# A fused Mamba, mixture-of-experts and attention kernel: the first scan's first B rows from TensorE, tables loaded ahead, filler products, orders set anew

## What is computed

```
x = x + mamba(layernorm(x))     # per sequence, a scan over 256 positions
x = x + moe(layernorm(x))       # router, top 2 of 8 experts
x = x + gated_attention(layernorm(x))
x = x + moe(layernorm(x))       # the same weights again
```

```
xn = x * rsqrt(mean(x * x) + 1e-6) * norm_scale
hidden, gate = split(xn @ in_w + in_b)
h = silu(causal_conv4(hidden) + conv_b)
ts, B, C = split(h @ xproj_w)              # 64, 16 and 16 columns
delta = softplus(ts @ dt_w + dt_b)
state_n[t] = exp(A_n * delta[t]) * state_n[t-1] + delta[t] * h[t] * B_n[t]
y[t] = sum_n C_n[t] * state_n[t] + D * h[t]
out = (y * silu(gate)) @ out_w + out_b
```

## Time and profile before

| | |
|---|---|
| median of 3 runs | 618.04 us (617.25 to 619.10) |
| the profiled execution | 618.93 us |
| its span in the trace | 617.1 us |
| TensorE granted clock, mean of the span | 0.986 |
| busy: TensorE, DVE, ScalarE, GpSimd | 595.6, 496.4, 396.9, 384.1 us |

### The profile page before, as it was taken

One profiled execution on the slowest core, in us unless ns is written; L12 is line 12 of the kernel. 1 busy time (PEld: TensorE's weight loads), 2 busy tenths in 40 slices (PEclk: granted clock), 3 DMA queues, 4 the chain that ended last, 5 costly groups with the idle time before them and its releaser, 6 DMA issues.

```text
span 617.1 us, 13011 instructions
## 1 busy us (share of the span) xinstructions
PE 595.6 (97%) x4502; PEld 550.9 (89%) x4502; DVE 496.4 (80%) x1077; ACT 396.9 (64%) x849; POOL 384.1 (62%) x360
## 2 busy tenths in 40 slices
PE   7779999799999999999999999999999999999997
PEld 6534886599999999999999999899999999999997
DVE  5796799788999899987999889898989895455444
ACT  5987777377677766867587767686676633616240
POOL 1494574579686997699678977697768773001000
PEclk9779999999999999999999999999999999999999
DMA  8763213101212204120404021210422000000000
GB/s 281 269 156 136 82 71 139 68 14 72 74 78 90 70 4 150 50 110 3 150 2 141 21 86 66 90 72 4 148 66 95 1 14 11 13 1 14 1 22 10
DMA packets 18466, 45.43 MB, mean 74 GB/s; under 512 B 2847, under 2 KB 13664, under 8 KB 14178
## 3 DMA queue, kind: packets, MB, share of 16 engines
q1 hardware_dynamic: 18402, 44.61, 21.0%
HBM read 40.15 MB, written 1.31 MB: 67 GB/s over the span
## 4 chain that ended last, share of the span: by engine, by line
PE 87%; POOL 3%; ACT 3%; issue 3%; DVE 2%; DMA 0%; SPq 0%; DVEq 0%; ACTq 0%; POOLq 0%
PE ps L1265 25%; PE ps L1069 14%; PE ps L1070 13%; PE ps L1071 13%; PE ps L1204 5%; PE ps L1314 2%; PE ps L1118 2%; POOL st L511 1%; POOL yacc L524 1%; PE ps L1084 1%; PE ps L1139 1%; PE ps L1064 1%; PE ps L1233 1%; PE ps L1326 1%; PE ps L1161 1%
## 5 line engine op out<-in xcount | busy, mean ns | idle before, releaser
L511 POOL TENSOR_TENSOR st<-st,rows_ring 128x512 f32<-128x512 f32 x128 | 164.0, 1285 | 85.6 <-DVE st L949 85.5
L1265 PE MATMUL ps<-down,inner_ring 128*128 128x128 f32 (+1 forms) x1408 | 171.5, 275 | 0.0
L1265 PEld LDWEIGHTS ps<-down,inner_ring 128*128 128x128 f32 (+1 forms) x1408 | 165.6, 191 | 2.6 <-issue 1.7
L750 ACT ACTIVATE sg<-ps 128x512 f32<-128x512 f32 x176 | 104.6, 596 | 82.5 <-PE ps L1071 72.5
L949 DVE TENSOR_TENSOR_SCAN st<-dA,ps 128x512 f32<-128x512 f32 x128 | 154.9, 1212 | 2.3 <-PE ps L1204 1.2
L1018 DVE TENSOR_TENSOR inner_ring<-sg,ps 128x512 f32<-128x512 f32 x176 | 119.1, 678 | 43.3 <-PE ps L1071 23.4
L524 POOL TENSOR_TENSOR yacc<-yacc,st 128x512 f32<-128x512 f32 x96 | 124.8, 1300 | 4.2
L698 ACT ACTIVATE dA<-delta,A 128x255 f32<-128x255 f32 x256 | 104.7, 495 | 0.2
L1069 PE MATMUL ps<-xhi,up_hi 128*128 128x256 f32 x352 | 103.9, 295 | 0.1
L1071 PE MATMUL ps<-xhi,up_lo 128*128 128x256 f32 x352 | 99.8, 283 | 0.0
L1070 PE MATMUL ps<-xlo,up_hi 128*128 128x256 f32 x352 | 99.7, 283 | 0.0
(11 more groups left out here) (150 smaller groups left out, 864.3 us busy)
## 6 DMA issues: line engine op xcount, KB each, us to landing
rows_ring<-bc SPq DMA_DIRECT2D x31, 1024.0 KB, 5.3
moved_rows<-inner_ring SPq DMA_DIRECT2D x96, 32.0 KB, 1.9
inner_ring<-gate_w SPq DMA_DIRECT2D x1, 1408.0 KB, 7.3
inner_ring<-up_w SPq DMA_DIRECT2D x1, 1408.0 KB, 10.0
down<-down_w SPq DMA_DIRECT2D x2, 512.0 KB, 10.4
out<-X SPq DMA_DIRECT2D x8, 128.0 KB, 1.9
rows_ring<-bc SPq DMA_DIRECT2D x1, 768.0 KB, 5.6
X<-x SPq DMA_DIRECT2D x1, 768.0 KB, 9.8
```

The source lines that it names most:

```text
L511: nc.gpsimd.tensor_tensor(st[:, i % NST], st[:, i % NST], row, ALU.mult).then_inc(s["m_p"], 1)
L750: nc.scalar.activation(sg[:, k % 2], two(bank_of(q, 2 * j)), ACT.Silu).then_inc(s["f_sg"], 1)
L1265: ins = nc.tensor.matmul(bank_of(q, 2 * NP + e)[:, c * H:(c + 1) * H], act_in, down[0:rows, e, n, :], start=n == 0, stop=n == NB - 1)
```

## The change

It changes five things in the code and all constants of the plan.

1. **B rows.** A new TensorE step `b_pe` takes, for states 0 and 1, the state's B column of `xproj_w` broadcast over 128 columns as the weights and h as the data, so the B row comes out on all 128 partitions in `rot[0]`. `dbx` of these two states copies it to SBUF (`b0`) first and no longer waits for the DMA; `mulC` of them waits for it, and the first sum waits until `rot[0]` is copied.
2. **Tables.** Two ScalarE steps, `t_soft` and `t_exp`, that only load a table.
3. **Fillers.** More in `m_turn` and `m_xp`, new ones before `m_dt` 0, `m_turn` 1, `m_ph` 1, `m_cv` 1 and before the sums 1 to 8 of sequence 0.
4. **Weight halves.** The second half of the weights' columns, which the first pairs use, is split first, and the first products wait for that half alone.
5. **Orders.** New constants, so new orders on every engine.

The code (the constants' tables but `TAPS` and `WARM` are left out; the orders that they give follow):

```diff
+NB0 = 2
+UP_PART = (3, 2, 0, 1)
...
-TAPS = {"split_in": 50.762, "lo_in": 60.743, "split_rows": 162.496, "lo_rows": 164.634, "h_table": 69.291}
-WARM = {"m_turn": 8, "m_ph": 2, "m_xp": 3, "sum": 2, "out": 6}
+TAPS = {"split_in": 37.063, "lo_in": 58.879, "split_rows": 161.491, "lo_rows": 172.175, "h_table": 65.824, "b_pe":
+        83.888, "t_soft": 75.704, "t_exp": 79.139}
+WARM = {"m_turn": 11, "m_ph": 2, "m_cv": 0, "m_xp": 5, "m_dt": 3, "turn1": 4, "ph1": 7, "cv1": 8, "early": 3, "sum":
+        2, "out": 6}
...
         delta = sb("delta", [P, 2, IT, T])
+        b0 = sb("b0", [P, NB0, T])
         rows_ring = sb("rows_ring", [P, NCH * CH * 2 * T])
...
                     pool.wait_ge(s["w_uh"], k // 2 + 1)
-                    cols = slice(k * HALF // 2, (k + 1) * HALF // 2)
+                    cols = slice(UP_PART[k] * HALF // 2, (UP_PART[k] + 1) * HALF // 2)
                     nc.gpsimd.tensor_tensor(up_lo[:, cols], up_raw[:, cols], up_hi[:, cols].bitcast(F32),
...
                 pool.wait_ge(s["m_scan"], i + 1)
+                if u == 0 and n < NB0:
+                    pool.wait_ge(s["d_r0" if n else "d_rf"], 16)
                 row = rowsbc[:, (i // CH) % NCH, n % CH, 1:2, :].broadcast_to([P, IT, T])
...
                     act.wait_ge(s["d_gate"], 16)
-                    half = slice(k * HALF, (k + 1) * HALF)
+                    half = slice((1 - k) * HALF, (2 - k) * HALF)
                     nc.scalar.copy(gate_hi[:, half], gate_raw[:, half]).then_inc(s["w_gh"], 1)
...
                     act.wait_ge(s["d_up"], 16)
-                    half = slice(k * HALF, (k + 1) * HALF)
+                    half = slice((1 - k) * HALF, (2 - k) * HALF)
                     nc.scalar.copy(up_hi[:, half], up_raw[:, half]).then_inc(s["w_uh"], 1)
...
                     dve.wait_ge(s["w_gh"], k + 1)
-                    half = slice(k * HALF, (k + 1) * HALF)
+                    half = slice((1 - k) * HALF, (2 - k) * HALF)
                     nc.vector.tensor_tensor(gate_lo[:, half], gate_raw[:, half], gate_hi[:, half].bitcast(F32),
...
                 dve.wait_ge(s["m_dx"], u + 1)
-                if i == 0:
-                    dve.wait_ge(s["d_rf"], 16)
+                if i < NB0:
+                    dve.wait_ge(s["m_b0"], i + 1)
                 else:
...
                 row = rowsbc[:, g % NCH, n % CH, 0:1, :].broadcast_to([P, IT, T])
+                if i < NB0:
+                    nc.vector.tensor_copy(b0[:, n], two(rot[0])[:, n]).then_inc(s["m_bc"], 1)
+                    dve.wait_ge(s["m_bc"], n + 1)
+                    row = b0[:, n:n + 1, :].broadcast_to([P, IT, T])
                 nc.vector.tensor_tensor(states_in(u, n), dxps, row, ALU.mult).then_inc(s["m_dbx"], 1)
...
                     dve.wait_ge(s["f_dn"], NE * (q - 1) + last_reader(j) + 1)
+                elif j >= RP + 2:
+                    dve.wait_ge(s["w_ul"], 4)
                 nc.vector.tensor_tensor(inner[:, j], sg[:, k % 2], two(bank_of(q, 2 * j + 1)), ALU.mult).then_inc(s["f_in"], 1)
...
+            summed = []
+
+            def fill(count):
+
+                if not summed:
+                    free("chain")
+                    warm(chainps, count)
+                elif summed[-1] < NS - 1:
+                    add_zeros(rot[0], count)
+
             def m_turn(u):
...
                     warm(chainps, WARM["m_turn"])
+                elif u == 1:
+                    fill(WARM["turn1"])
                 free(bank_name(u))
...
                     warm(chainps, WARM["m_ph"])
+                elif u == 1:
+                    fill(WARM["ph1"])
                 free(bank_name(u))
...
                     return
+                fill(WARM["cv1" if u else "m_cv"])
                 pe.wait_ge(s[f"w_diag{0 if u else 1}"], 1)
...
+            def b_rows(_):
+
+                pe.wait_ge(s["d_xpw"], 16)
+                pe.wait_ge(s["m_h"], 1)
+                for n in range(NB0):
+                    for it in range(IT):
+                        col = xpw[:, it, 96 + 2 * n:97 + 2 * n].broadcast_to([P, P])
+                        ins = nc.tensor.matmul(two(rot[0])[:, n], col, h[:, it], start=it == 0, stop=it == IT - 1)
+                    ins.then_inc(s["m_b0"], 1)
+
             def m_dt(u):
                 if u == 0:
+                    fill(WARM["m_dt"])
                     pe.wait_ge(s["d_dtw"], 16)
...
                     pe.wait_ge(s["m_y0"], u + 1)
+                    if u == 0:
+                        pe.wait_ge(s["m_bc"], NB0)
                     nc.tensor.matmul(two(rot[0]), ident[:], yacc[:, u % 2], start=True, stop=False)
+                summed.append(n + u * NS)
                 if n > NS // 2:
                     add_zeros(rot[0], WARM["sum"])
+                elif n and u == 0:
+                    add_zeros(rot[0], WARM["early"])
                 pe.wait_ge(s["m_p"], i + 1)
...
                     pe.wait_ge(s["m_scan"], NS)
-                    pe.wait_ge(s["w_gl"], 2)
+                    pe.wait_ge(s["w_gl"], 1)
                 elif q == 0 and 2 * j < NR0:
...
                     pe.wait_ge(sem, value)
+                if q == 0 and j == RP:
+                    pe.wait_ge(s["w_gl"], 2)
                 if j:
...
                 if q == 0 and j == 0:
-                    pe.wait_ge(s["w_ul"], 4)
+                    pe.wait_ge(s["w_ul"], 2)
                     pe.wait_ge(s["m_delta"], 2)
...
                     pe.wait_ge(sem, value)
+                if q == 0 and RP <= j < RP + 3:
+                    pe.wait_ge(s["w_ul"], 3 if j == RP else 4)
                 products(bank_of(q, 2 * j + 1), (up_hi, up_lo), q, j).then_inc(s["f_U"], 1)
```

94 lines of the change are left out of this document (47 added, 47 removed).

## The result

The kernel after takes 611.29 us (median of 5 executions, 610.72 to 612.87), beside 617.61 for before: ratio 0.990, interval 0.9881 to 0.9919, so **6.3 us faster**. Measured again later it took 611.73 against 618.15 (ratio 0.9913, 0.9882 to 0.9944).

A forecast was written before the change was run, and what follows sets the result against it. TensorE, busy 97% of the span, was taken to bound the kernel. Gains of 0.9 + 1.0 + 0.5 + 0.6 = 3.0 us took the execution from 618.93 to 615.9, the median to 615.0; range 612.2 to 618.5.

The forecast's parts named there:

- step 6: Later stages: moving `lo_rows` gains 0.5 us, less waiting of `m_out` 2 gains 0.6, all other later moves 0.
- Step 1: Kernel start: 22 filler pieces in place of 16 may raise the clock before the convolution; h 1.4 us earlier.
- Steps 2 and 3: Front up to sequence 0's scan: tables and B rows, then the scan, whose last state ends at 51.8, 0.9 us earlier.
- step 2: Delta's end to first scan: tables ahead and B rows on TensorE gain nothing, +0.2 us.
- Step 4: End of sequence 0's sums: TensorE loaded to the brim, last sum at 56.7 where before had 57.61, gain 0.9 us.
- Step 5: Behind scan 0: `m_dx` 1 and dbx (1, 0) move into DVE's wait, gain 1.3 us, 0.3 lost elsewhere, net 1.0.
- B: More than forecast: half clock at 120 to 130 us absent, whole 1.25 us wait gone; 612.2 us, chance 0.18.
- A: Front: TensorE's chain pays the gain back, fillers only fill, the wait at 182 stays; 616.9 us, chance 0.20.
- C: Front: ScalarE's `m_h` 1 waits for `m_cv` 1, ending near 35, so scan 6 starts late; 619.9 us, chance 0.10.
- D: Later 495 us: moves on packed engines lose what the front gains; 618 +/- 1 us, chance 0.06.

The follow-up runs named there:

- pace3: The kernel before with only the places of sequence 2's scan as in after, in the order all engines share; median 617.82 us.
- after_again: The kernel after, unchanged, measured again later: 611.73 us against 618.15 for before.
- no_bpe: The kernel after with the first two states' B rows by DMA again; first scan at 21.62 us, median 1.9 us above after's, intervals meeting.

## Why the prediction was wrong

**What failed** is the last term of step 6: "All other later moves stay under packed TensorE: 0, bounds -1 to +1." They gave 2.8 us in the distances from the fourth stage on, 2.8 times that bound. It rested on stretches with 10.00 of 10 busy, and that is no proof of a packed engine where rows overlap. I had read one idle piece of 1.25, where the distances hold 11.5 us, of which other orders take 4.1 away: 1.5 ahead of `m_out`, and 2.6 in pieces of up to 0.4, mostly where TensorE waits for ScalarE's normed rows and for a stage's or Mamba's first product.

**Also in step 6**, `m_out` 2's wait was put at 0.6, the middle of its bounds. All of it went, and the third to fourth stage is 1.4 shorter; pace3 gives 1.0 for the same move alone. `lo_rows` was put at 0.5. The wait at 82.59 is gone in after, but the first to second stage is 0.2 shorter only: undersized by 0.8, oversized by 0.3.

**Step 1** had the mechanism in the profile: the convolution product takes 1.97, the clock is 1.00 to 50 us, and h's second half comes 2.2 us earlier where 1.4 was forecast. Its cause, more fillers, holds as a matter of how often: with 22 pieces the product ran at full clock in 12 of 12 profiles, with 16 in 2 of 8. Its reason, that TensorE has no break, isn't shown: in those two the clock rose at 5.1 and 5.8 and the break from 5.3 on was not closed. And part of the 2.2 is luck of the pair, since the moment differs by execution (4.5 in after, 6.2 in after_again).

**Steps 2 and 3** held. Delta's end to the first scan took 4.88 (forecast 4.75, before 4.59), `lo_rw` 1.03 (0.7), the wait for decay (0, 6) 0.55 (0.4), the last scan ended at 51.01 (51.8, off by step 1's 0.7). The 0.2 that step 2 lost, for tables and B rows together, came out as 0.3; within the new orders B rows on TensorE are worth 0.3 at the first scan (no_bpe), where I had the part that names the change gain nothing. Of the Trainium skill's drain of 1.38 us behind each table load (ScalarE: Activation LUTs, What ACT_TABLE_LOAD costs) nothing shows: scan 6 waited 0.55, not 2.8 more, and the load at 16.02, 1.28 long, is followed by `m_norm` at 17.32, 0.02 behind its end. That GpSimd's reads slow a small DVE instruction (SBUF — State Buffer, Who interferes with whom) fits: `lo_rw` took 0.80 to 1.53 in the 20 profiles, and in each it ends 0.02 to 0.03 behind the GpSimd instruction beside which it started (35.02 and 35.00 in after).

**Step 4** was low by 0.8 (gain 1.67, forecast 0.9), nearly all of it from step 1's earlier chain. "Loaded to the brim" was right: DVE waited 3.64 us for the last sum, and the fillers ahead of the sums cost 1.1 between the first scan and the last sum.

**Step 5** held as a part: 1.25 measured, 1.3 forecast. The net was 0.7 (7.30 from `m_gate` to the first expert product before, 6.59 after) where I had 1.0.

**The rivals.** B's first half came about, the spell of half clock at 120 to 130 us (1.5 in the profiled pair), but as luck of an execution: five of after's eleven have a mean clock that fits one spell, and take 1.9 us more. A (TensorE pays it back), C (ScalarE behind `m_cv` 1, which ended at 26.2 and not near 35) and D (later orders cost) fell. By the distances, the pair of profiles is 2.3 + 0.2 + 1.5 + 1.4 + 2.8 against my 1.9 + 0.5 + 0 + 0.6 + 0. The medians' 6.3 is less than 8.2, since before's profiled execution was 1.3 above its median of 617.61, and after's 0.6 below its own.

## What to carry to other kernels

Where rows of one engine overlap, test a stretch that reads 10.00 of 10 by the distances between starts: the spacing of the same products elsewhere is the yardstick. Count on from the product before and not from row to row, since behind a slower product a row starts early and lasts longer, and neither that distance nor a mean duration is a wait. An order by hand over five in-order queues is one object: price it whole and place by place in the plan that all engines share, not by engine; here a part taken over alone cost three to six times what the whole brought. And compare distances between markers in two profiles before medians, since spells of low clock come and go by execution.
